# A wavelet-attention block on one core: the order of one slot, a second gate buffer, another order of the start, two bank pairs in the head, and a tail that adds x by DMA

## What is computed

```python
ll, lh, hl, hh = haar_dwt(x)                 # 80 x 80 each
wav = concatenate([ll, lh, hl, hh], axis=1)  # 1024 channels
fused = relu(bn(conv1x1(wav, fusion_w)))     # 256 channels
sp_in = [mean over channels, max over channels]
spatial_out = sigmoid(conv7x7(sp_in)) * fused
ch_map = sigmoid(mlp(mean over pixels) + mlp(max over pixels))
projected = relu(bn(conv1x1(ch_map * spatial_out, proj_w)))  # 1024 channels
return haar_idwt(projected) + x
```

## Time and profile before

| | us |
|---|---|
| Median of 3 runs | 2432.77 |
| Lowest and highest | 2432.01, 2437.65 |
| The profiled execution's own time | 2437.94 |
| Its span in the trace | 2436.1 |

### The profile page before, as it was taken

How to read it: one execution, slowest core, us unless ns; L and a number is a source line. 1 busy time by engine, 2 the same in 40 slices (tenths; PEclk the granted TensorE clock), 3 DMA queues, 4 the chain that set the end, 5 groups by cost and what they waited for, 6 DMA issues and landing times. The chain is left out here.

```text
span 2436.1 us, 30288 instructions
## 1 busy us (share of the span) xinstructions
PE 2318.6 (95%) x11109; PEld 2046.7 (84%) x11109; DVE 2146.2 (88%) x2774; ACT 1088.8 (45%) x1441; POOL 524.1 (22%) x491
## 2 busy tenths in 40 slices
PE   6999999999999999999999999999999999997897
PEld 5787789888898888988898888989789888885786
DVE  6877889898889988899888998889989898889898
ACT  3445544454444544455343544445444453434432
POOL 0111111111111111111111111111111111147899
PEclk9999999999999999999999999999999999998999
DMA  4455699999999999999999999999999999997798
GB/s 161 159 180 194 189 281 297 279 301 267 284 280 289 284 276 268 293 286 294 271 281 275 300 269 277 294 277 282 287 269 294 281 293 276 275 278 264 277 346 318
DMA packets 112616, 660.54 MB, mean 271 GB/s; under 512 B 17682, under 2 KB 18772, under 8 KB 112212
## 3 DMA queue, kind: packets, MB, share of 16 engines
q1 hardware_dynamic: 86260, 488.21, 52.4%
q0 software_dynamic: 26208, 170.41, 37.8%
HBM read 448.24 MB, written 210.33 MB: 270 GB/s over the span
## 5 line engine op out<-in xcount | busy, mean ns | idle before, releaser
L511 PE MATMUL pp<-y_hi,wp_hi 128*128 128x480 f32 (+1 forms) x1792 | 679.0, 379 | 62.3 <-DVE sd L821 49.6
L535 PE MATMUL pfs<-x_hi,wf_hi 128*128 128x480 f32 (+1 forms) x1792 | 668.7, 373 | 17.8 <-DVE x_lo L775 14.7
L511 PE MATMUL pp<-y_lo,wp_hi 128*128 128x480 f32 (+1 forms) x1792 | 673.0, 376 | 0.0
L511 PE MATMUL pp<-y_hi,wp_lo 128*128 128x480 f32 (+1 forms) x1792 | 671.2, 375 | 0.0
L535 PE MATMUL pfs<-x_lo,wf_hi 128*128 128x480 f32 (+1 forms) x1792 | 665.0, 371 | 0.0
L535 PE MATMUL pfs<-x_hi,wf_lo 128*128 128x480 f32 (+1 forms) x1792 | 664.8, 371 | 0.0
L598 ACT ACTIVATE x_hi<-xin 128x1920 fp32r<-128x1920 f32 (+1 forms) x224 | 419.5, 1873 | 476.2 <-PE pfs L535 471.7
L775 DVE TENSOR_TENSOR x_lo<-xin,x_hi 128x1920 fp32r<-128x1920 f32 (+1 forms) x224 | 461.6, 2061 | 169.3 <-ACT x_hi L598 169.3
L626 ACT ACTIVATE relu<-pp,t 128x480 f32<-128x480 f32 (+1 forms) x448 | 287.2, 641 | 396.7 <-PE pp L511 373.0
L427 POOL DMA_DIRECT2D xre<-in_x_dram x182 | 159.9, 879 | 1380.7 <-DVE xre L838 1380.7
L511 PEld LDWEIGHTS pp<-y_hi,wp_hi 128*128 128x128 f32 x1792 | 342.8, 191 | 117.3 <-DVE sd L821 60.4
(11 more groups left out here) (94 smaller groups left out, 1236.3 us busy)
## 6 DMA issues: line engine op xcount, KB each, us to landing
xin<-in_x_dram SPq DMA_DIRECT2D x160, 960.0 KB, 7.4
out_dram<-xre SPq DMA_DIRECT2D x160, 960.0 KB, 5.7
xre<-in_x_dram POOLq DMA_DIRECT2D x130, 960.0 KB, 9.6
xin<-in_x_dram SPq DMA_DIRECT2D x64, 800.0 KB, 7.4
out_dram<-xre SPq DMA_DIRECT2D x64, 800.0 KB, 5.3
xre<-in_x_dram POOLq DMA_DIRECT2D x52, 800.0 KB, 9.6
xre<-in_x_dram SPq DMA_DIRECT2D x30, 960.0 KB, 7.2
sigb<-sig_scratch SPq DMA_DIRECT2D x56, 400.0 KB, 8.0
```

The costliest lines, as they stand in the source:

```text
L511: mm = pe.matmul(pp[j][:, 0:n_px], w[:, kt, cols], y[:, s.pc, kt, 0:n_px], start=(kt == 0 and m == 0), stop=(kt == CT - 1 and m == 2))
L535: mm = pe.matmul(pf[o][:, 0:n_px].rearrange("p (y w) -> p y w", w=W2), w[:, i, q, o * P:(o + 1) * P], v[:, q % 2, :, q // 2, :], start=(i ...
```

## The change

1. **LAST.** In phase 7 DVE runs `butterflies(s, 0)`, `cells`, and `lower` of the next tile ahead of `channel_max`, `x_lower(k+1, 1)` and `turn`.
2. **Gate chunks.** Two buffers, `sigb` and a part of `xre`'s fourth buffer, so each chunk is loaded after the chunk two before it. The output ring has three buffers until slot 111 (`home`) and four in the tail.
3. **Start.** DVE runs the butterflies on the unscaled weights as soon as they land; ACT applies the scale behind them (`fhs_ready`). Only the scale of the fusion is computed first; that of the projection, its weights and biases follow x's split. PE transposes each half when it is there, and starts each q of its first fusion when that q's `wf_lo` is there.
4. **Head.** Odd slots from 3 to 19 fuse into `pp[0]` and `pp[1]`, so a fusion waits for the slot two before it. Where the pair changes, the split of x's second half goes ahead of the drain on ACT and of `channel_max` on DVE.
5. **Tail.** In slots 114 to 117 `cells` write to `xre` and POOL adds x with the accumulating DMA.

```diff
+        gates = [sigb[:, :], xre[:, RING - 1, 0:CPX]]
+        def other(k):
+            return 3 <= k < LAG and k % 2 == 1
+        def before(k):
+            return max((j for j in range(max(k - 3, 0), k) if other(j) == other(k)), default=-1)
+        def bank(k, o):
+            return (pp if other(k) else pf)[o]
         def adding(kc, i):
-            return kc + LAG < NT
+            return kc + LAG < NT or kc + LAG - NT in GATED
+        THREE = 2 * (NT - LAG)
+        home = [g % 3 for g in range(THREE)]
+        tail_homes = [3] + home[-3:]
+        home += [tail_homes[g % 4] for g in range(2 * LAG)]
...
             def load_sig(s, c):
-                need(sp, mult_done, CT * (NCH * s.nb + c))
-                sp.dma_start(sigb[:, :], ...).then_inc(sigb_landed, 16)
+                need(sp, mult_done, CT * (NCH * s.nb + max(c - 1, 0)))
+                sp.dma_start(gates[c % 2], ...).then_inc(sigb_landed[c % 2], 16)
...
@@ SP body
-                    load_sig(s, GATED[s.phase][0])
+                    if GATED[s.phase][0] == 0:
+                        load_sig(s, 0)
+                    load_sig(s, GATED[s.phase][1])
...
-                if s.phase in GATED and s.a:
-                    load_sig(s, GATED[s.phase][1])
+                if s.phase in GATED and s.a and GATED[s.phase][1] + 1 < NCH:
+                    load_sig(s, GATED[s.phase][1] + 1)
...
@@ PE, start and fusion
-            pe.wait_ge(fh_ready, 8)
-            for q in range(4):
-                for i in range(CT):
-                    for o in range(CT):
+            for o in range(CT):
+                pe.wait_ge(fhs_ready, o + 1)
+                for q in range(4):
+                    for i in range(CT):
...
-            pe.wait_ge(wflo_ready, 4)
+                if s.k == 3 and i == 0:
+                    pe.wait_ge(wplo_ready, 4)
+                    if s.k == 0 and i == 0:
+                        pe.wait_ge(wflo_ready, q + 1)
-                            need(pe, f_ready, CT * (s.k - 1) + o + 1)
+                        if i == 0 and q == 0 and before(s.k) >= 0:
+                            pe.wait_ge(f_ready, CT * before(s.k) + o + 1)
...
@@ ACT, start
+            x_upper(0, 0)
+            for o in range(CT):
+                act.wait_ge(scale_ready, 1)
+                act.wait_ge(fh_ready, 4 * (o + 1))
+                nc.scalar.activation(fh[:, o, :, :], fh[:, o, :, :], ACT.Copy, scale=t1[:, 2, o:o + 1]
+                                     ).then_inc(fhs_ready, 1)
...
@@ DVE, start
+            def haar(o):
+                w = tmp if o == 0 else tmp2
+                for j in range(2):
+                    nc.vector.tensor_tensor(w[:, 2 * j, :], fw[:, o, 2 * j, :], fw[:, o, 2 * j + 1, :], ALU.add)
+                    ins = nc.vector.tensor_tensor(w[:, 2 * j + 1, :], fw[:, o, 2 * j, :], fw[:, o, 2 * j + 1, :],
+                                                  ALU.subtract)
+                link(ins)
...
+            dve.wait_ge(w_landed, 16)
+            haar(0)
             dve.wait_ge(v_psum, 1)
...
+            scale_and_bias(v1, slice(0, CT))
+            haar(1)
+            x_lower(0, 0)
+            for q in range(4):
+                dve.wait_ge(wfhi_ready, q + 1)
...
+            x_lower(0, 1)
+            scale_and_bias(v2, slice(CT, CT + NB))
...
@@ DVE body
+                if ahead:
+                    butterflies(s, 0)
+                    cells(s, 0)
+                    if s.c_next:
+                        lower(s.kn)
+                if s.load_next and other(s.k) != other(s.k + 1):
+                    x_lower(s.k + 1, 1)
                 if s.a:
                     channel_max(s)
-                if s.load_next:
+                if s.load_next and other(s.k) == other(s.k + 1):
                     x_lower(s.k + 1, 1)
```

More of the change, by code:

```diff
@@ L281, in span_of, with turns @@
             return block, block * GROUP, (FIRST[t] + ROWS[t]) * W2 - block * GROUP
+        THREE = 2 * (NT - LAG)
+        home = [g % 3 for g in range(THREE)]
+        tail_homes = [3] + home[-3:]
+        home += [tail_homes[g % 4] for g in range(2 * LAG)]
+        def turns(g):
+            return sum(home[n] == home[g] for n in range(g))
         def uses(g, by_dma):
-            return sum(adding(*divmod(n, 2)) == by_dma for n in range(g % RING, g + 1, RING))
+            return sum(home[n] == home[g] and adding(*divmod(n, 2)) == by_dma for n in range(g + 1))
         def pooled(kc):
@@ L396, in _ @@
             for p in range(RING):
-                sp.wait_ge(stored[p], 16 * len(range(p, 2 * NT, RING)))
+                sp.wait_ge(stored[p], 16 * home.count(p))
         @block.gpsimd
@@ L457, in body @@
                     channel_sum(s)
+                if s.c_next and not s.next_is_first and pooled(s.kn) and not s.a:
+                    lower(s.kn)
                 if s.c and adding(s.kc, 0):
@@ L605, in _ @@
                                      ACT.Copy).then_inc(wfhi_ready, 1)
-            for i in range(CT):
-                x_upper(0, i)
+            x_upper(0, 1)
             def prepare_late():
+                act.wait_ge(bias_ready, 3)
                 for q in range(4):
@@ new lines, in _, with prepare_late @@
+            haar(1)
+            x_lower(0, 0)
+            for q in range(4):
+                dve.wait_ge(wfhi_ready, q + 1)
+                nc.vector.tensor_tensor(wf_lo[:, :, q, :], pp[q][:, :].rearrange("p (i o) -> p i o", i=CT),
+                                        wf_hi[:, :, q, :].bitcast(F32), ALU.subtract).then_inc(wflo_ready, 1)
+            def prepare_late():
+                for q in range(4):
+                    dve.wait_ge(wphi_ready, q + 1)
+                    cols = slice((q % 2) * 512, (q % 2 + 1) * 512)
+                    nc.vector.tensor_tensor(wp_lo[:, q // 2, cols], pp[q][:, :], wp_hi[:, q // 2, cols].bitcast(F32),
+                                            ALU.subtract).then_inc(wplo_ready, 1)
@@ L803, in butterflies @@
                 n_px = px_of(s.kc)
-                if s.a and (i == 1 or s.phase == LAST):
+                if s.a and i == 1:
                     dve.wait_ge(turned_ready, s.k + 1)
@@ L952, in body @@
                     lower(s.kn)
-                if ahead:
-                    butterflies(s, 0)
-                    cells(s, 0)
-                    if s.c_next:
-                        lower(s.kn)
                 if s.c:
```

112 lines of the change are left out of this document (48 added, 64 removed).

## The result

The changed kernel takes 2395.03 us (median of 4 runs, 2393.21 to 2397.32) beside 2435.0 for the kernel before on the same chip: a ratio of 0.9828, 95% interval 0.9805 to 0.9851. Measured a second time beside its variants it gave 0.9807 (0.9784 to 0.9829). The profiled execution took 2397.32 us, its span is 2395.4.

A forecast was written before the change was run, and what follows sets the result against it. PE was taken to bound the steady part, with a few DVE stalls, and DVE the gated tail. Terms 9.9 + 3 + 19 + 9 + 10 = 51 us off the median 2432.8 gave 2382, range 2367 to 2404.

The forecast's parts named there:

- Start, 9.9: Before PE's first fusion matmul: it starts at 17.6 instead of 27.48 us, gaining 9.9 us.
- Head, 3: Slots 1 to 13: a second pair of banks removes waits for the drain in slots 9 to 14, gaining 3 us.
- "nothing" happened in slots 2 to 8: Head slots 2 to 8: DVE's work of 11.7 us against PE's 10.5 stays, so these slots gain nothing.
- Bounds of 0 and -6: Head: the range given for the change in time, from no gain to 6 us less.
- LAST, 19: Slot LAST of the images: PE's stall before the projection goes, 13 us, and clock falls behind it, 6 us.
- 13 with the restart: LAST: stalls of 2.0 us with the restart in six images and 1.1 in the first, 13 us in all.
- Gate chunks, 9: Steady part: DVE's waits for gate chunks go, 7 us of them reaching PE, plus 2 for the clock.
- the 7 of the step: Gate chunks: of DVE's 12.2 us of waits for chunks, 7 were counted as reaching PE over six images.
- Tail, 10: Slots 114 to 117: gates without POOL's sums gain 9.6 us; two residual loads leaving SP's queue gain 0.5.
- their new wait for a stored buffer is hidden: Tail: the wait of `cells` for a stored buffer costs nothing, four homes giving 28 us against about 19.
- Ring of three, 0: Output ring: three buffers cost nothing, with 18.8 us to a free buffer against 31.5 between uses.

The follow-up runs named there:

- the pair of runs: Changed kernel with one gate buffer loaded at the old places: 0.9854 with the ring of three, 0.9829 with the old ring of four; ratios to the kernel before.

## Why the prediction was right, and where it was off

The time was in the range, and the order of the parts held. The gain was over-estimated, 51 against 44: 2 to 3 us too much each at the head, at LAST and in the tail. By its steps, each with what undoing it cost or, for the start, what its rows show:

- *Start, 9.9.* 27.48 less 17.86 is 9.6; no run undoes it. The scale stood at 11.57 and ACT's second scaling ended at 15.61, as the sum had them.
- *Head, 3.* The mechanism was half right. The drains' waits went, but not "nothing" happened in slots 2 to 8: DVE's lateness, before spread over eight waits, now came at every second tile in waits of up to 2.1 us, and the clock fell. Slots 9 to 14 gained 2.3 us where the step had 3. In all, two pairs are worth 2.0 less 1.7 for the fall; by the times, one pair costs 0.6 us, which is far inside the uncertainty. Bounds of 0 and -6 left no room for a loss of clock.
- *LAST, 19.* No wait of a projection for `sd` is left behind LAST. Undoing it costs 16.7: 12.3 for the waits as counted, where the step had 13 with the restart, and 3.4 for the clock in place of 6. The falls behind LAST do go, but in the changed kernel others stand behind the waits of 1.76 that remain, so part of what a fall cost is not saved but moved.
- *Gate chunks, 9.* Undoing it costs 8.9. PE's waits for `sd` outside LAST are 10.6 in place of 17.8, the 7 of the step. For the clock the step had 2; in the profiled executions its falls cost 6.9 more with one buffer, so this part moves from one execution to the next.
- *Tail, 10.* The size is 6.9, and two errors hide in it. The gates run from their first to their last in 49.3 us in place of 59.0: 9.7, foreseen as 9.6. The DVE instructions fall from 1.674 and 1.491 us to 0.984 when POOL's sums leave. This agrees with the section "Who interferes with whom" of the page "SBUF — State Buffer" of the Trainium skill, by which a DVE instruction with two inputs in SBUF contends with a POOL instruction that reads SBUF. Ahead of the gates 4.4 us were won, where the step had 0.5: the loads of the gates are issued 2.7 us behind the store of the sigmoid in place of 7.3 (rows below), and with the tail undone it is 7.8 again. So the residual loads ahead of that store, the last of them issued 0.5 us before it, are most likely what slowed it; no run takes them alone away. Behind the gates 7.2 are lost: 11.49 of PE's waiting in place of 4.28 (9.53 in the second trace of the changed kernel). The step that failed is "their new wait for a stored buffer is hidden". It looked at DVE's wait in the slots that add. It did not follow SP, which in the same order has stores that now wait for adds and then the first load of the slot behind, nor POOL, on which `lower` stands behind that slot's sum.
  SP's rows of the changed kernel (L378 is the store of the sigmoid, L418 the loads of the gates) and of the kernel before:

```profile
2151.45 0.34 SPq L378 DMA_DIRECT2D sig_scratch<-sig  x1
2154.12 0.33 SPq L418 DMA_DIRECT2D x_lo<-sig_scratch  x1
```

```profile
2186.62 0.43 SPq L330 DMA_DIRECT2D xre<-in_x_dram  x1
2187.15 0.85 SPq L350 DMA_DIRECT2D sig_scratch<-sig  x1
2194.44 0.32 SPq L388 DMA_DIRECT2D x_lo<-sig_scratch  x1
```

- *Ring of three, 0.* No wait for a store appears, but the pair of runs leaves up to a few us open.

Together 9.6 + 0.6 + 16.7 + 8.9 + 6.9 = 42.7, against 44 measured. Four of these terms are uncertain by 5 to 6 us each, so that they meet within 2 us is partly luck.

The best version is the changed kernel with slot 118 added by DMA as well: 0.9795 beside 0.9828 and 0.9807, and 2 us of it seen in the traces.

## What to carry to other kernels

When some groups of a ring change from one way of filling to another, price the border. The last group of the one kind and the first of the other share an in-order queue, and every instruction behind the first is late by what the last one waits. A wait that is taken away by reordering may only change its name (POOL's sum became ACT's split): add up the engine's whole work beside what runs at the same time, and take that tile's length, not the mean. And waits that are gathered into fewer, longer ones can cost more than their sum.

## What the hardware showed

Each single fall of the granted clock, from 2.4 to 1.2 GHz by its level, costs 1.7 us. Up to 2140 us it comes behind waits of PE of 1.3 to 3.0 us. Three waits of 2.9 to 3.5 us of the kernel with one gate buffer brought falls of twice the cost (12 us from 818 us at a granted clock of 0.72: 3.4 us). A fall does not come behind each wait: of the six waits of 1.86 us of LAST in the kernel before four brought one. The waits of 1.76 us stand at the same six places in both traces of the changed kernel; falls followed at 821, 1394 and 1681 us in the one and at 530, 1104 and 1677 in the other. The fourth fall of the first trace, at 725 us, stands behind a wait of 1.34 us for the convolution's maps. The 48 first fusion matmuls took 12.73 us in the first and 11.44 in the kernel with LAST's old order, while both show a granted clock of 1.00 (changed kernel first):

```profile
20.00:24.00 4.00, 4.00 (x15) 3.41 (x14) 3.48 (x9) 0.31 (x1) 0.00 (x0) 1.00 0.31 73
```

```profile
20.00:24.00 4.00, 4.00 (x20) 3.44 (x19) 3.49 (x9) 0.30 (x1) 0.00 (x0) 1.00 0.22 60
```

15 against 20 matmuls in the same 4 us: at the start the column does not show all of the slower clock. The two traces of the changed kernel are 7.6 us apart. Up to 2140 us the first has two falls more, 3.4 us; another 3.6 us arise behind the last fusion matmul, where the gates start 2 us later and the stall behind them is 2 us longer (11.49 against 9.53), and why is not shown.
